# Layer 0 of a four-layer expert network: scaling in place, first expert weights loaded ahead of the routing, expert numbers read once a tile, rows turned first

## What is computed

```python
def _L0_ffn_ref(hidden_states, gate_w, shared_gate_w, shared_up_w, shared_down_w, routed_gate_w, routed_up_w, routed_down_w):
    x = hidden_states.reshape(-1, h)                              # 2048 x 256
    shared_out = _swiglu(x, shared_gate_w, shared_up_w, shared_down_w)
    logits = x @ gate_w                                           # 32 experts
    topk_ids = jnp.argmax(logits, axis=-1)
    scores = jax.nn.sigmoid(jnp.max(logits, axis=-1))[:, None]
    xs = x * scores
    order = jnp.argsort(topk_ids)
    sorted_x = xs[order]
    g = _grouped_mm(sorted_x, routed_gate_w, tokens_per_expert)   # 256 x 512 for each expert
    u = _grouped_mm(sorted_x, routed_up_w, tokens_per_expert)
    d = _grouped_mm(jax.nn.silu(g) * u, routed_down_w, tokens_per_expert)
    return (shared_out + d[jnp.argsort(order)]).reshape(b, s, h)
```

## Time and profile before

| | us |
|---|---|
| three timed runs | 1874.29, 1870.13, 1861.41 |
| the profiled execution: its own time | 1879.61 |
| its span in the trace | 1877.9 |
| `half_l0`, in the trace | from 57 to about 388 |
| the routed experts in it | from 119.5 to about 332 |
| PE busy in the whole span | 1508.4 (80%) |
| DVE, ACT, POOL busy | 972.7, 660.2, 315.6 |
| mean granted TensorE clock | 0.895 |

### The profile page before, as it was taken

One profiled execution on the slowest core, in us unless ns is written; L12 is line 12 of the kernel. 1 busy time (PEld: TensorE's weight loads), 2 busy tenths in 40 slices (PEclk: granted clock), 3 DMA queues, 4 the chain that ended last, 5 costly groups with the idle time before them and its releaser, 6 DMA issues. The chain is left out here.

```text
span 1877.9 us, 26047 instructions
## 1 busy us (share of the span) xinstructions
PE 1508.4 (80%) x8186; PEld 1133.1 (60%) x8186; DVE 972.7 (52%) x1703; ACT 660.2 (35%) x981; POOL 315.6 (17%) x327
## 2 busy tenths in 40 slices
PE   3758787867679999887999999999965898518992
PEld 2533333633558777766788888887754776405662
DVE  2626677352353435463677777774542333325775
ACT  1327676211032333332555555553321232102110
POOL 0520000300034005143000000002407004230003
PEclk9979999887579999989999999999986999658996
DMA  6058982112042223025112222201122222136623
GB/s 195 17 207 314 353 314 76 57 53 91 2 156 101 68 88 118 25 79 221 45 58 104 90 90 88 113 15 51 57 90 97 93 89 87 34 111 242 236 104 109
DMA packets 75799, 213.18 MB, mean 114 GB/s; under 512 B 9696, under 2 KB 47984, under 8 KB 67472
## 3 DMA queue, kind: packets, MB, share of 16 engines
q1 hardware_dynamic: 52672, 152.20, 22.6%
q0 software_dynamic: 17952, 54.15, 8.6%
q10 hardware_dynamic: 5040, 5.11, 0.8%
HBM read 164.90 MB, written 46.53 MB: 113 GB/s over the span
## 5 line engine op out<-in xcount | busy, mean ns | idle before, releaser
L843 DVE TENSOR_TENSOR sb_h_split<-sb_big,sb_h_split 128x2048 fp32r<-128x2048 f32 x78 | 178.3, 2288 | 83.7 <-ACT sb_h_split L838 83.7
L838 ACT CAST sb_h_split<-sb_big 128x2048 fp32r x78 | 148.1, 1902 | 37.0 <-issue 36.0
L978 ACT COPY sb_g_space<-sb_big 128x1024 f32 x120 | 118.5, 1046 | 75.0 <-DMA sb_big<-in_l_routed 46.3
L978 DVE COPY sb_g_space<-sb_big 128x1024 f32 x168 | 108.4, 693 | 67.4 <-issue 38.8
L734 PE MATMUL ps<-sb_big,sb_e_hT 128*128 x624 | 141.0, 379 | 1.1 <-DVE sb_e_hT L887 1.1
L270 PE MATMUL ps<-sb_h_split 128*128 128x512 f32 x312 | 134.6, 432 | 8.7 <-DVE sb_h_split L862 5.9
L270 PE MATMUL ps<-sb_g_split,sb_g_ws 128*128 128x512 f32 x256 | 109.0, 426 | 28.5 <-DVE sb_g_product L449 17.4
L734 PEld LDWEIGHTS ps<-sb_big,sb_e_hT 128*128 128x128 f32 x624 | 118.2, 190 | 18.5 <-issue 1.3
L272 PE MATMUL ps<-sb_h_split 128*128 128x512 f32 x312 | 123.4, 396 | 0.0
L271 PE MATMUL ps<-sb_h_split 128*128 128x512 f32 x312 | 122.8, 393 | 0.0
L1014 PE MATMUL ps<-sb_g_space,sb_e_rT 128*32 128x512 f32 x768 | 97.1, 623 | 24.0 <-ACT sb_e_rT L1068 12.8
(11 more groups left out here) (387 smaller groups left out, 3232.5 us busy)
## 6 DMA issues: line engine op xcount, KB each, us to landing
sb_big<-in_l_routed SPq DMA_DIRECT2D x32, 1024.0 KB, 6.2
sb_big<-in_l2f_routed SPq DMA_DIRECT2D x8, 3072.0 KB, 11.4
sb_e_wring<-in_l_experts SPq DMA_DIRECT2D x16, 1408.0 KB, 6.4
sb_big<-in_l_routed SPq DMA_DIRECT2D x32, 512.0 KB, 7.3
sorted_out<-sb_big POOLq DMA_DIRECT2D x22, 512.0 KB, 4.5
sb_big<-sorted_in SPq DMA_DIRECT2D x18, 512.0 KB, 3.9
sorted_out<-sb_big SPq DMA_DIRECT2D x18, 512.0 KB, 2.9
sb_big<-sorted_in POOLq DMA_DIRECT2D x15, 512.0 KB, 10.6
```

Source lines behind the costliest of these rows:

```text
L838: act.copy(self.own[part][:, 0, :], self.raw(e, part)).then_inc(self.own_high[part], 1)
L843: dve.tensor_tensor(self.own[part][:, 1, :], self.raw(e, part), self.own[part][:, 0, :], ALU.subtract).then_inc(self.own_low[part], 1)
L978: last = copy(self.own[part][:, g, :], here.rearrange("p s n -> p (s n)"))
```

## The change

1. POOL scales tiles 0 to 7 only, in place in `ctok`. DVE scales tiles 8 to 15, in place, two after each of the first four up parts' `hidden_low` (`beside`, called in `dve_jobs` with m = 0 to 3). POOL's indirect DMAs go out of `ctok`, and those of tiles 8 to 15 wait for the tile's scaling on DVE.
2. The up ring lies on FCOL2 and EXTRA, the down ring on CTOK. With that SP issues up 0 to up 3 at the start of the block, and waits for `known` and `sent` only ahead of down 0 (`ready`).
3. ACT and DVE read the numbers of their lanes' experts once a round (`experts_of`: two reads on ACT, three on DVE, for 5 and 7 before). On ACT they stand ahead of `copy_rows`, on DVE behind the copy of the turned hidden rows, in both ahead of the part's wait.
4. ACT copies the turned rows of round 0 ahead of its fills. Part 2 of round 0 is filled within the loop, behind parts 0 and 1 of round 1, on both engines.

```diff
--- before.py
+++ after.py
@@ -485,7 +485,7 @@
                         between(n - 2)
                 self.hidden_high(act, self.NF * n1 - 1)
 
-            def dve_jobs(self, dve, n0, n1, between=None):
+            def dve_jobs(self, dve, n0, n1, between=None, beside=None):
 
                 for m in range(self.NF * n0, self.NF * n1):
                     n, f = divmod(m, self.NF)
@@ -494,6 +494,8 @@
                     self.multiply(dve, m)
                     if m > self.NF * n0:
                         self.hidden_low(dve, m - 1)
+                    if beside is not None:
+                        beside(m)
                     if f == self.NF - 1:
                         if n > n0:
                             self.add(dve, n - 1)
@@ -913,15 +915,14 @@
         class LaneExperts:
 
 
-            def __init__(self, tag, on, halves, lanes, weights, region, space, rows, slots, glu, hT):
+            def __init__(self, tag, on, halves, lanes, weights, region_up, region_down, space, rows, slots, glu, hT):
 
                 self.halves, self.lanes, self.weights, self.rows, self.rounds = halves, lanes, weights, rows, rows.tiles
                 self.tile_expert, self.last_round = slots.tile_expert, slots.last_tile
                 self.NE, self.NF, self.F, self.W = weights.shape[0], halves * FU // P, halves * FU, P // lanes
                 self.KF, self.FD = KD * self.F, self.NF * D
-                ends = lanes * 2 * self.KF
-                self.ring_up = region[:, 0:ends].rearrange("p (r n) -> p r n", r=lanes)
-                self.ring_down = region[:, ends:ends + lanes * self.FD].rearrange("p (r n) -> p r n", r=lanes)
+                self.ring_up = region_up.rearrange("p (r n) -> p r n", r=lanes)
+                self.ring_down = region_down.rearrange("p (r n) -> p r n", r=lanes)
                 self.own = [space[:, n * lanes * self.KF:(n + 1) * lanes * self.KF].rearrange("p (g n) -> p g n", g=lanes)
                             for n in range(3)]
                 self.sg, self.h, self.hT = glu.sg, glu.product, hT
@@ -949,42 +950,43 @@
                 to = (self.ring_up, self.ring_down)[down]
                 sp.dma_start(to[:, e % self.lanes, :], self.weights[e][:, lo:hi]).then_inc(arrived[r], 16)
 
-            def load_weights(self, sp):
+            def load_weights(self, sp, ready):
 
                 sp.sem_inc(self.up_in[1], 1)
                 sp.sem_inc(self.down_in[1], 1)
                 for e in range(self.NE + self.lanes - 1):
                     if e < self.NE:
                         self.load_part(sp, e, 0)
+                    if e == self.lanes - 1:
+                        ready(sp)
                     if e >= self.lanes - 1:
                         self.load_part(sp, e - self.lanes + 1, 1)
 
-            def fill(self, eng, copy, r, part, lanes, own):
+            def fill(self, eng, copy, r, part, lanes, own, experts):
 
                 if r >= 1:
                     eng.wait_ge((self.gate, self.up, self.downed)[part], r if part == 2 else r * self.halves)
-                arrived = (self.up_in, self.up_in, self.down_in)[part]
-                places = []
-                for g in lanes:
-                    q = r * self.lanes + g
-                    e = eng.value_load(self.tile_expert[0:1, q:q + 1], min_val=0, max_val=self.NE - 1)
-                    places.append(bass.ds(e % self.lanes, 1))
                 if part != 1:
+                    arrived = (self.up_in, self.up_in, self.down_in)[part]
+                    e = experts[max(lanes)]
                     eng.wait_ge(arrived[0], (e // 2 + 1) * 16)
                     eng.wait_ge(arrived[1], ((e + 1) // 2) * 16 + 1)
-                for g, place in zip(lanes, places):
+                for g in lanes:
+                    place = bass.ds(experts[g] % self.lanes, 1)
                     here = (self.ring_up[:, place, 0:self.KF], self.ring_up[:, place, self.KF:2 * self.KF],
                             self.ring_down[:, place, :])[part]
                     last = copy(self.own[part][:, g, :], here.rearrange("p s n -> p (s n)"))
                 last.then_inc(own[part], 1)
 
-            def fill_act(self, act, r, part):
-                lanes = {4: ((2, 3), (2, 3), (3,)), 2: ((1,), (1,), (1,))}[self.lanes][part]
-                self.fill(act, act.copy, r, part, lanes, self.act_own)
-
-            def fill_dve(self, dve, r, part):
-                lanes = {4: ((0, 1), (0, 1), (0, 1, 2)), 2: ((0,), (0,), (0,))}[self.lanes][part]
-                self.fill(dve, dve.tensor_copy, r, part, lanes, self.dve_own)
+            def experts_of(self, eng, r, lanes):
+                return {g: eng.value_load(self.tile_expert[0:1, r * self.lanes + g:r * self.lanes + g + 1],
+                                          min_val=0, max_val=self.NE - 1) for g in lanes}
+
+            def fill_act(self, act, r, part, experts):
+                self.fill(act, act.copy, r, part, ((2, 3), (2, 3), (3,))[part], self.act_own, experts)
+
+            def fill_dve(self, dve, r, part, experts):
+                self.fill(dve, dve.tensor_copy, r, part, ((0, 1), (0, 1), (0, 1, 2))[part], self.dve_own, experts)
 
             def wait_own(self, pe, r, part):
                 pe.wait_ge(self.act_own[part], r + 1)
@@ -1072,19 +1074,21 @@
                 act.copy(self.rows.tile(r), psum[:, 7, 0:D]).then_inc(self.outc, 1)
 
             def act_tiles(self, act, between=None):
-                for part in range(3):
-                    self.fill_act(act, 0, part)
+                experts = self.experts_of(act, 0, (2, 3))
                 self.copy_rows(act, 0)
+                self.fill_act(act, 0, 0, experts)
+                self.fill_act(act, 0, 1, experts)
                 for r in range(self.rounds):
-                    more = r + 1 < self.rounds
+                    now = experts
                     self.silu(act, r)
-                    if more:
+                    if r + 1 < self.rounds:
+                        experts = self.experts_of(act, r + 1, (2, 3))
                         self.copy_rows(act, r + 1)
-                        self.fill_act(act, r + 1, 0)
-                        self.fill_act(act, r + 1, 1)
+                        self.fill_act(act, r + 1, 0, experts)
+                        self.fill_act(act, r + 1, 1, experts)
                     if r >= 1:
                         self.result(act, r - 1)
-                        self.fill_act(act, r, 2)
+                    self.fill_act(act, r, 2, now)
                     if between is not None:
                         between(r)
                 self.result(act, self.rounds - 1)
@@ -1097,14 +1101,16 @@
                     dve.tensor_copy(self.hT[u % 2][:, :], psum[:, 4 + u % 2, :]).then_inc(self.hid_c, 1)
 
             def dve_tiles(self, dve, between=None):
-                for part in range(3):
-                    self.fill_dve(dve, 0, part)
+                experts = self.experts_of(dve, 0, (0, 1, 2))
+                self.fill_dve(dve, 0, 0, experts)
+                self.fill_dve(dve, 0, 1, experts)
                 for r in range(self.rounds):
-                    more = r + 1 < self.rounds
+                    now = experts
                     if r >= 1:
                         self.turned_hidden(dve, r - 1)
-                    if more:
-                        self.fill_dve(dve, r + 1, 0)
+                    if r + 1 < self.rounds:
+                        experts = self.experts_of(dve, r + 1, (0, 1, 2))
+                        self.fill_dve(dve, r + 1, 0, experts)
                     for u in range(r * self.halves, (r + 1) * self.halves):
                         dve.wait_ge(self.up, u + 1)
                         dve.wait_ge(self.silud, u + 1)
@@ -1112,10 +1118,9 @@
                             dve.wait_ge(self.hid_t, u - 1)
                         dve.tensor_tensor(self.h[:, u % 2, :], self.sg[:, u % 2, :], psum[:, 2 + u % 2, :], ALU.mult
                                           ).then_inc(self.hidden, 1)
-                    if more:
-                        self.fill_dve(dve, r + 1, 1)
-                    if r >= 1:
-                        self.fill_dve(dve, r, 2)
+                    if r + 1 < self.rounds:
+                        self.fill_dve(dve, r + 1, 1, experts)
+                    self.fill_dve(dve, r, 2, now)
                     if between is not None:
                         between(r)
                 self.turned_hidden(dve, self.rounds - 1)
@@ -1327,9 +1332,9 @@
 
 
             with ExitStack() as own:
-                rows = as_tokens(fx)
                 jobs, split = [(0, 0), (0, 1), (0, 2), (0, 3)], 2
-                order, sent, scaled, mixed = (sem("h0_" + n) for n in ("order", "sent", "scaled", "mixed"))
+                order, sent, scaled, scaled_dve, mixed = (
+                    sem("h0_" + n) for n in ("order", "sent", "scaled", "scaled_dve", "mixed"))
                 got = [sem(f"h0_got{c}") for c in range(NCH)]
 
```

(29 more changed lines are left out.)

## The result

The changed kernel takes 1854.56 us (median of 10 runs, 1847.01 to 1859.88), and the kernel before 1875.18 us (10 runs, the three shown above among them). The ratio is 0.9894, with a 95% interval of 0.9866 to 0.9921: 1.06% faster, and 20.6 us by the medians. (A ratio here is worked out over all runs of both kernels and is not the quotient of the two medians.) The forecast was 1840, the range 1825 to 1859. The span of the profiled execution is 1855.0 us, 22.9 less than before.

The account below looks back on a forecast made before the run. Bound in turn by PE's shared expert, ACT's rows' copy behind a wait for down weights, then rounds of 8.16 us. Gains 8.1 + 10.7 + 11.1 = 29.9 us, 1870.1 to 1840; range 1825 to 1859.

Parts of the forecast that it names:

- two of the rivals: Reads are not DVE's idle gap (1851 us, chance 0.05); DVE's scalings each hold a scatter (1851 us, chance 0.07).
- Scaling and scatter: Shared expert's down products: earlier scatter shrinks PE's gaps, down(1) ends at 110.6 instead of 118.7; gain 8.1 us.
- DVE holds the scatters: Rival, scatter: each of DVE's eight scalings holds a scatter 2.2 us, sent at 117.8; 1851 us, chance 0.07.
- Weights ahead, rows first: Start of round 0: first gate 4.2 us after down(1) instead of 14.0; gain 10.7 us, between 9 and 12.
- term 1: Shared expert's down products, from earlier scaling and scatter: gain 8.1 us, no less than 2, no more than 10.
- The 0.9 for the clock: First gate of round 0: PE's clock may still be high after a shorter idle; 0 to 1.7 us, 0.9 taken.
- The reads: Expert rounds: fewer reads remove DVE's idle ahead of part 2; late rounds 3.2, end 1.9, middle 6 us.
- slower rival: Every round: grouped reads exposed on DVE ahead of part 0, 9.8 us a round; 24 us slower, 1894, chance 0.03.
- The middle, 6 us: Silu 0 to silu 19, rounds partly waiting for weights: reads gain between 0 and 15 us, 6 taken.
- a sign of being wrong: Silu 0 to silu 19: the forecast is wrong if the period stays at 8.16 us a round.
- weight-stream rival: From up 4 on the weight stream is the bound: only 12.8 us gained, 1857 us, chance 0.15.
- the prediction's first rival: down(0): PE's gaps stay, perhaps from its own instruction supply; gain there only 2 us, 1846, chance 0.15.

Follow-up runs that it names:

- held scatter: Changed kernel with POOL's scatter held until both down products of the shared half are done: 1855.33 us in one run, against 1853.78 for the changed kernel beside it.
- group B: Follow-up runs sharing one chip: kernel before 1834.12 us, changed kernel 1804.49 (ratio 0.9843), plus variants of the changed kernel.
- rows last: Changed kernel with the order of round 0 undone: all three parts filled ahead of the loop, ACT's copy of the turned rows behind them; 1815.44 us, ratio 0.992.
- reads spread: Changed kernel with expert numbers of round r+2 read one at a time behind running fills, not three in a row: 1801.44 us, ratio 0.9833.
- the two kernels on the reads: Kernel before with only the once-a-round reads added, 1826.56 us (0.9977); changed kernel with each part reading its own numbers again, 1813.08 us (0.9907).

## Why the prediction was right, and where it was not

The direction was right and the time lies in the range, 15 us above the point. 5 of the 15 are the kernel before, whose median over ten runs is 1875.2 and not 1870.1. The other 9 are gain that did not come: 20.6 us of 29.9, nearer to what two of the rivals had (18.8 and 19.4) than to the forecast. The wide range, and not each term, is what held. Step by step:

*Scaling and scatter.* POOL's eight scalings took 7.85 for 7.9. The scatter began 18.9 into the block for 18.2 forecast, and ended 41.6 (last issue) for 40.2. The first one took 3.16, the length that the prediction took over from the scaling at 75.94 of the earlier trace rows. `down(1)` ended 2.0 later than forecast: 1.8 us of pauses stayed, and a lower clock behind them. Busy times inside `down(0)` of the kernel after, as in the earlier trace rows:

```profile
100.00:104.00 4.00, 2.21 (x14) 1.82 (x14) 1.41 (x3) 1.72 (x3) 1.97 (x3) 0.98 0.20 72
104.00:108.00 4.00, 2.94 (x14) 2.64 (x13) 1.60 (x3) 0.00 (x0) 2.51 (x4) 0.60 0.93 283
```

I had tied the pauses to POOL's last issue, and left 1.2 us of them. But they lie from 101.2 to 103.7 there, mostly behind the end of that issue (101.7), and before they went on to 107.0, behind it too (106.1). They end about when the scatter has landed and SP's next load goes (103.21; 107.64 before). The held scatter shows that without a scatter there are none; it shows no more of the mechanism.

*DVE holds the scatters.* Three scatters beside a pair of DVE's scalings (and, in part, other DVE work) took 1.64, 1.41 and 1.19 for 0.96, 1.4 us together, not 2.2 for each scaling. The first scatter had seven DVE operations beside it, a pair of scalings among them, and what each adds to its 3.16 is not told apart. The other three are 0.2 to 0.7 longer, each beside a pair of scalings (0.60 us); by what mechanism, no run shows.

*Weights ahead, rows first.* "The gate 4.2 us after `down(1)`" was exact. The split of the gain was not. I took the 14.0 us between `down(1)` and the first gate of before as a cost that follows `down(1)`. In group B `down(1)` of the kernel before ends 9.8 us earlier, and its first gate comes at 75.4, where it was on the first chip (75.3). It hung on `sent`, 25 us before it, and the loads behind that. So term 1 was worth nothing while the old order stood, and became worth its full size with the new one: the terms were not independent, only their sum was right (15.9 for 18.8 on the first chip, 20.1 on that of group B). Weights ahead, which I named first, gives about 2 us; rows first gives 9 to 11. Of the 10.5 between the first gate of before and that with rows last (75.4 to 64.9), what the earlier scatter gives and what the weights ahead was not told apart. The 0.9 for the clock did not come: but for one turn of rows PE had waited since `down(1)`, 4.2 us for 14.0, and the gate took 3.64 at a granted clock of 0.50, as before (3.62 at 0.53).

*The reads.* The gain in late rounds was 1.1 for 3.2. The mis-sized term is the period before: I took 7.17 from two DVE rows, while the silus 19 to 23 are 27.0 / 4 = 6.75 apart; the period after, 6.45, is near the 6.4 that I had named. And the reads did not vanish in their new place, 1.0 to 1.5 us ahead of part 0 stayed as idle time; "DVE's round becomes 5.8" came true only with the reads spread (5.9). The slower rival saw the place rightly, at too high a price. At the end it was 4.0 for 1.9; the two kernels on the reads put 2.8 and 3.2 of it down to them.

*The middle, 6 us.* It gave 3.0 (1.3 in group B), a period of 8.0 for 8.16, which is close to what I had named as a sign of being wrong. The stream did start earlier, up 4 by 4.4 us and up 5 by 14.5 (forecast 7.7 and 19), and the rounds did not follow it. I put the waits there down to the share of the DMA engines, 0.89 of 1, and so to bytes. That step failed. The earlier trace rows already showed ACT waiting 6.92 us for down weights, a load of 0.5 MB, while the engines were busy with 1 MB loads asked for ahead of it, and three quarters of ACT's waits for weights and most of DVE's were for down weights. An earlier start of the stream and fewer reads change nothing of that order; two issues of SP exchanged gave 10.5 us of the 24 that wait for weights. The weight-stream rival had the right place; its mechanism, the bytes, can be the rest at most.

## What to carry to other kernels

Where a queue of loads has several kinds, look which kind the consumers wait for, and which wait stands ahead of its issue: behind a share of 0.9 on the DMA engines there were 10.5 us to gain by the order alone (with the reads spread as well, PE's busy share went from 0.80 to 0.86 and that of the DMA engines from 0.91 to 0.95). Ahead of a stage's first matmul, do first what another engine still has to work on (here one copy of 0.37 us ahead of 4 us of fills and of a wait for down weights, 9 to 11 us). Reading fewer numbers ahead of a wait helped here only as far as the remaining reads stood behind running work (silu 19 to 23 in group B: 28.1 us before, 25.8 with three reads in a row, 23.6 with one at a time).

## What the runs showed of the hardware

- The kernel before takes 1875, 1833, 1834 and 1870 us (medians) in four groups of runs on three chips or more, at mean granted clocks of 0.894 to 0.909. Between its two traces (clocks 0.895 and 0.902) about 45 us of the difference (1545.1 and 1500.3) lie behind the block studied; within it, silu 0 to silu 19 took 155.1 and 152.2.
- POOL's indirect DMAs beside dense matmuls make the end of the matmuls 3.6 us later on one chip (54.9 for 51.3, one trace of each) and not measurably on others (51.3 to 51.5 with them), with no semaphore of the program between them. The first profiles named PE's pauses "issue", and with the scatter held there is no pause. What PE waits for in those of 1.8 and 4.4 us beside a scatter, and whether it is what the prediction's first rival names, no run shows.
- A number read into a register costs DVE 0.305 + 0.19 us and ACT 0.276 + 0.15 (medians of 72 and 48 in the kernel after), and three in a row ahead of a copy left 1.0 to 1.5 us of idle time, while one at a time behind running copies left 0.2 to 0.3.
